# A fused recurrent block and six attention layers on one core: the half step's instructions in a new order on all five engines

## The reference, cut to what matters

```python
xn = layernorm(x)                      # x: (2, 1024, 128)
s = recurrent(xn)                      # 192 hidden channels, scan over the tokens
y = xn
for i in range(6):                     # 16 heads of 64, windows of 32 tokens
    q, k, v = split(shift_tokens(y) @ Wqkv[i])        # 128 -> 3 x 1024
    q, k = rotary(l2norm(q) * qs[i]), rotary(l2norm(k) * ks[i])
    att = softmax(mask(q @ k.T * 8)) @ v   # each window looks at itself and the one before
    y = att @ Wo[i] + y
    h = layernorm(shift_tokens(y)) @ W1[i] + b1[i]    # 128 -> 2 x 341
    y = (h[:341] * gelu(h[341:])) @ W2[i] + b2[i] + y
out = x + s * silu(y)
```

## Time and profile before

| | us |
|---|---|
| median of 3 runs | 1771.38 |
| the runs | 1769.56, 1771.38, 1780.35 |
| the profiled execution, its own time | 1782.22 |
| its span | 1780.4 |
| TensorE busy | 1595.2 (90%) |
| VectorE busy | 1417.4 (80%) |
| GpSimd busy | 1367.1 (77%) |
| ScalarE busy | 1070.2 (60%) |

### The profile page before, as it was taken

One profiled execution on the slowest core, in us unless ns is written; L12 is line 12 of the kernel. 1 busy time (PEld: TensorE's weight loads), 2 busy tenths in 40 slices (PEclk: granted clock), 3 DMA queues, 4 the chain that ended last, 5 costly groups with the idle time before them and its releaser, 6 DMA issues.

```text
span 1780.4 us, 76109 instructions
## 1 busy us (share of the span) xinstructions
PE 1595.2 (90%) x32303; PEld 1327.5 (75%) x32303; DVE 1417.4 (80%) x2163; ACT 1070.2 (60%) x2132; POOL 1367.1 (77%) x1321
## 2 busy tenths in 40 slices
PE   6888898999999898998999888899899999999986
PEld 3767777777777787777877777777777777777865
DVE  7777788778778687778888777888877899998964
ACT  5545565656656565566665656666665666666752
POOL 7877888878779677778877778887787967767732
PEclk9999999999999899899999999999999999999988
DMA  4334332434333334232343333243333333332330
GB/s 135 88 79 106 76 88 67 102 88 109 72 90 76 82 86 117 66 84 71 91 104 91 91 80 88 68 114 89 96 80 81 85 74 71 85 77 62 75 88 27
DMA packets 217857, 151.20 MB, mean 85 GB/s; under 512 B 144557, under 2 KB 164657, under 8 KB 217521
## 3 DMA queue, kind: packets, MB, share of 16 engines
q1 hardware_dynamic: 217520, 146.33, 33.7%
HBM read 27.50 MB, written 1.05 MB: 16 GB/s over the span
## 4 chain that ended last, share of the span: by engine, by line
PE 32%; SPq 29%; DVE 17%; DMA 10%; issue 8%; ACT 2%; POOL 1%; DVEq 0%; ACTq 0%; POOLq 0%
DMA v_win<-v_new 10%; SPq L608 9%; PE ps_pv L868 7%; SPq L606 4%; DVE ss L1523 4%; SPq L603 4%; DVE v_new L1534 4%; PE ps_pv L890 3%; SPq L294 3%; PE ps_qn L777 3%; SPq L574 3%; PE ps_tr L802 2%; PE ps_s L842 2%; PE ps_qn L779 2%; PE ps_qn L778 2%
## 5 line engine op out<-in xcount | busy, mean ns | idle before, releaser
L1976 POOL TENSOR_TENSOR qk<-qk,t 128x1024 f32<-128x1024 f32 x192 | 459.0, 2392 | 135.1 <-DVE qk L1513 134.9
L1510 DVE TENSOR_TENSOR t<-ps_qn,tab 128x512 f32<-128x512 f32 x384 | 263.7, 687 | 149.3 <-ACT sq L1164 142.3
L1988 POOL TENSOR_TENSOR qkr<-qk,rinv 128x1024 f32<-128x1024 f32 x192 | 364.0, 1917 | 7.6 <-POOL rinv L1968 0.2
L777 PE MATMUL ps_qn<-w_hi,xs_hi 128*128 128x512 f32 x576 | 268.0, 465 | 46.1 <-DVE v_new L1534 35.6
L1164 ACT ACTIVATE sq<-ps_qn 128x512 f32<-128x512 f32 x384 | 231.5, 603 | 89.8 <-PE ps_qn L779 89.4
L868 PEld LDWEIGHTS ps_pv<-pT,v_win 64*64 64x64 f32 x12288 | 208.5, 140 | 91.9 <-issue 91.6
L1513 DVE TENSOR_TENSOR qk<-ps_qn,tab 128x512 f32<-128x512 f32 x384 | 261.4, 681 | 0.0
L868 PE MATMUL ps_pv<-pT,v_win 64*64 64x32 f32 x12288 | 230.7, 225 | 12.3 <-issue 10.4
L779 PE MATMUL ps_qn<-w_hi,xs_lo 128*128 128x512 f32 x576 | 236.2, 410 | 0.0
L778 PE MATMUL ps_qn<-w_lo,xs_hi 128*128 128x512 f32 x576 | 235.8, 409 | 0.4 <-issue 0.4
L1534 DVE COPY v_new<-ps_qn 128x512 f32<-128x512 f32 x184 | 119.6, 686 | 133.1 <-DMA v_win<-v_new 127.6
(11 more groups left out here) (169 smaller groups left out, 3002.5 us busy)
## 6 DMA issues: line engine op xcount, KB each, us to landing
v_win<-v_new SPq DMA_DIRECT2D x576, 128.0 KB, 2.4
v_win<-v_new SPq DMA_DIRECT2D x192, 64.0 KB, 2.1
v_win<-v_win SPq DMA_DIRECT2D x188, 64.0 KB, 2.0
kT<-kT SPq DMA_DIRECT2D x84, 128.0 KB, 3.1
w_raw<-in_Wqkv SPq DMA_DIRECT2D x18, 512.0 KB, 4.7
rot<-in_rot SPq DMA_DIRECT2D x48, 128.0 KB
wo<-in_Wo SPq DMA_DIRECT2D x6, 512.0 KB, 4.3
x<-x SPq DMA_DIRECT2D x48, 56.0 KB
```

What stands on the lines that cost most here:

```text
L777: mm(ps_qn[bank][:, :], xs_hi[b][:, :], w_hi[:, part], start=True, stop=False)
L1510: v.tensor_tensor(t2[:, part].rearrange("p (h s d) -> p h s d", s=2, d=DH // 2), swapped, tab[:, 2 * k + 1:2 * k + 2, :].rearrange("p o (s ...
L1976: g.tensor_tensor(qk[b][:, part], qk[b][:, part], t2[:, part], ALU.add).then_inc(added[b], 1)
L1988: g.tensor_tensor(qkr[b][:, part].rearrange("p (h d) -> p h d", d=DH), qk[b][:, part].rearrange("p (h d) -> p h d", d=DH), rinv[b][:, k * ...
```

## The change

- **v in two places**: `v_new` has two buffers for each stream, by the step's parity. `evac_v` is ScalarE's now, in all steps, and waits for the moves of tile i-2 instead of those of tile i-1.
- **Half step in a new order**: on TensorE the mask stands earlier and `scores` and both parts of `probs_v` follow each other at the end of the half. The mixed transpose stands just before them.
- **Output projection half a step later**: the projection of stream 1 of tile i-3 is done in half (i, 0), that of stream 0 of tile i-2 in half (i, 1), with the down products of tile i-4.
- **Up products** are done in half (i, 0) and fill the banks of `pv_order` instead of those of `qn_order`. All mixed transposes fill `tr_order`.
- **Engines**: `low_x` (L2037 before), `low_fxn` (L2006) and `normalise_mid` (L2012) are VectorE's instead of GpSimd's. On GpSimd `scale_probs` stands before the second `add`. On ScalarE `inverse_root` is the last of a half instead of the first.
- **SyncE** issues `move_v` of the half before first, then the shift of `xmid`.
- The drain is rewritten to match.

The core of the diff:

```diff
@@ pv_order
     for b in range(B):
+        if has_out(i, 1 - b):
+            order += [("out", 1 - b)]
+        if b == 0 and valid(i - 4):
+            order += [("up", c) for c in range(3)]
         if valid(i - 2):
-            order += [("pv", b, f) for f in range(2)]
-        if valid(i - 2) or (b == 0 and valid(i - 5)):
-            order += [("out", b)]
+            order += [("pv", b, h) for h in range(2)]
...
-        v_new = per_stream("v_new", [P, INNER])
+        v_new = [[sb(f"v_new{b}_{n}", [P, INNER]) for n in range(2)] for b in range(B)]
...
@@ SyncE, half
                     if b == 0:
+                        carry_k(i, 1)
+                        move_v(i - 1, 1)
+                        shift_xmid(i)
                         load_out_weights(i)
-                        shift_xmid(i)
+                    else:
+                        carry_k(i + 1, 0)
+                        move_v(i, 0)
...
-                    carry_k(i, b)
-                    move_v(i, b)
...
@@ TensorE, half
                     qkv(i, b, (0, 1))
...
-                    probs_v(i, b, 0)
+                    out_projection(i, 1 - b)
+                    if b == 0:
+                        ffn_up(i, 0)
+                    transpose_keys(i, b)
                     mask(i, b)
-                    probs_v(i, b, 1)
                     qkv(i, b, (2, 3))
...
+                    rec_hidden(i, b)
+                    rec_gate_projection(i, b)
                     if b == 0:
-                        ffn_down(i)
-                        transpose_keys(i, b)
+                        ffn_up(i, 1)
...
+                    transpose_qk(i, b, 0)
+                    rec_output(i, b)
+                    rec_rates(i, b)
+                    transpose_qk(i, b, 1)
+                    qkv(i, b, (4, 5))
...
+                    if b == 0:
+                        ffn_up(i, 2)
+                    if not i.first:
                         transpose_mixed(i, b)
...
                     scores(i, b, 0)
                     scores(i, b, 1)
+                    probs_v(i, b, 0)
+                    probs_v(i, b, 1)
...
@@ ScalarE, evac_v
-                    if i.n > 1:
-                        return
                     bank, n = fill(qn_order, i, ("qkv", b, c))
                     act.wait_ge(qn_full[bank], n)
-                    if c == 4:
-                        after_first(act, v_moved[b], i.n * V_MOVE, i)
-                    f(v_new[b][:, (c - 4) * COLS:(c - 3) * COLS], ps_qn[bank][:, :], ACT.Copy).then_inc(qn_done[bank], 1)
+                    if c == 4 and valid(i - 2):
+                        act.wait_ge(v_moved[b], (i.n - 1) * V_MOVE)
+                    f(v_new[b][i.n % 2][:, (c - 4) * COLS:(c - 3) * COLS], ps_qn[bank][:, :], ACT.Copy).then_inc(qn_done[bank], 1)
...
@@ VectorE, half
+                        if c == 1:
+                            take_out(i, 1 - b)
+                            row_sums(*soft)
+                            row_recips(*soft)
+                            if b == 0:
+                                rec_driving(i - 1, 1)
+                            else:
+                                normalise_rows(i)
...
-                        evac_v(i, b, 4)
-                        evac_v(i, b, 5)
-                        if i.t == 4:
+                        ffn_gate(i, 2)
+                    if not (i.first and b == 0):
+                        low_x(*next_tile(i, b))
+                    if b == 0:
+                        mid_variance(i)
+                    else:
+                        low_fxn(i - 3)
...
@@ GpSimd, half
-                    if b == 1:
-                        low_fxn(i)
                     add(i, b, 0)
-                    if b == 1:
-                        normalise_rows(i)
...
+                    scale_probs(*softmax_tile(i, b))
                     add(i, b, 1)
-                    scale_probs(*softmax_tile(i, b))
-                    if not early(*next_tile(i, b)):
-                        low_x(*next_tile(i, b))
```

More of the change, by code:

```diff
@@ L139, in tr_order @@
         if valid(i - 1):
-            order += [("qk", b, f) for f in (2, 3)]
-        if b == 1 and has_mixed(i, b):
-            order += ["mixed"]
-        if valid(i - 1):
-            order += [("qk", b, f) for f in (0, 1)]
+            order += [("qk", b, f) for f in (2, 3, 0, 1)]
+        if has_mixed(i, b):
+            order += [("mixed", b)]
     return order
@@ L193, in fill @@
 def fill(order, i, what):
-    steps = sum(len(order(Step(0, k))) for k in range(min(i.n, STEPS)))
-    n = steps + (order(i).index(what) if i.n < STEPS else DRAIN_FILLS[order].index((i.n, what)))
+    first = sum(len(order(Step(0, k))) for k in range(min(i.n, STEPS)))
+    n = first + (order(i).index(what) if i.n < STEPS else DRAIN_FILLS[order].index((i.n, what)))
     return n % 2, n // 2 + 1
@@ L206, in down_of, with mixed_of @@
     return "down" if i.n >= STEPS else ("out", 0)
+def mixed_of(i, b):
+    return "mixed" if i.n >= STEPS else ("mixed", b)
 def build(nc, a):
@@ L568, in shift_xmid @@
                         return
[L569 to L570 removed]
+                    wait_fill(sp, pv_done, pv_order, i - 1, ("out", 0))
+                    wait_fill(sp, pv_done, pv_order, i, ("out", 1))
                     k, to = mid_slot(n), slice(0, HALF)
@@ L743, in transpose_mixed @@
                         return
-                    order, full, done, banks = mixed_ring(b)
-                    bank, n = fill(order, i, "mixed")
-                    ring_free(pe, done, bank, n)
+                    bank, n = fill(tr_order, i, mixed_of(i, b))
+                    ring_free(pe, tr_done, bank, n)
                     t, s = next_tile(i, b)
@@ L1124, in evac_mixed @@
                         return
-                    order, full, done, banks = mixed_ring(b)
-                    bank, n = fill(order, i, "mixed")
-                    act.wait_ge(full[bank], n)
+                    bank, n = fill(tr_order, i, mixed_of(i, b))
+                    act.wait_ge(tr_full[bank], n)
                     t, s = next_tile(i, b)
-                    m = i - 4
+                    m = i - 3
                     if valid(t):
```

555 lines of the change are left out of this document (240 added, 315 removed).

## The result

| | median us | runs |
|---|---|---|
| before | 1775.87 | 4, 1769.56 to 1781.08 |
| after | 1968.49 | 4, 1962.57 to 1975.02 |

The ratio is 1.109 (95% interval 1.103 to 1.115): **slower by 11%**. The forecast was 1680, range 1600 to 1755, and its chance of slower was 0.09, given to a mechanism that did not occur. The profiled execution after took 1975.0, its span 1972.9.

The account below looks back on a forecast made before the run. Bound: a loop through v's copy, SyncE's queue and DMA, 35.1 us a step. New step 31.1 + 0.4 + 1.5 = 33.0; 39 x 2.1 plus 8 recurrent x 1.2 gives 92 us less: 1680, range 1600 to 1755.

Parts of the forecast that it names:

- the loop: Each step cycled through VectorE's copy of v, SyncE's queue and the move DMAs, 35.1 us on average; two buffers break it.
- Tiled products together: Scores and `probs_v` in one run on TensorE: six tiling switches become three a half, saving 0.7 us a step.
- TensorE's work of 31.1 us a step: Floor of an ordinary step: TensorE's measured 31.8 us less 0.7 for fewer tiling switches.
- The wait for rotations: In half (i, 1) TensorE waits for late VectorE before the last chunk: 2.0 us lost, 1.5 counted.
- the third gate's wait: Near the end of half (i, 0) TensorE waits 0.4 us for the third gate, behind the 2.2 us of `ss`.
- The recurrent steps: Eight steps with the recurrence, 38.7 us each before: gain between 0 and 2.3 us, middle 1.2 taken.
- Rival 2: VectorE's four moved places wait for GpSimd's running instructions, 3.9 us a step: 1816 us, slower; chance 0.09.
- Rival 3: ScalarE's loaded half with b = 0 runs 2 us late, a new loop keeping the step at 35.1: 1771 us; chance 0.10.
- Rival 1: ScalarE and VectorE hand on in time, only TensorE's work of 31.1 us a step is left: 1597 us; chance 0.14.

Follow-up runs that it names:

- the best version: Kernel before with v in two places and the mask behind both parts of `probs_v`, plus ScalarE copying v in all steps: 1646.4 us, ratio 0.929.
- The kernel at 1792: Kernel after with the scores and last up chunk ahead of the fifth chunk, and the recurrence's matmuls behind both query transposes: 1792.2 us, ratio 1.011.
- the kernel at 1675: Kernel before with v in two places and the mask behind both parts of `probs_v` instead of between them, VectorE still copying v: 1675.4 us, ratio 0.941.

## Why the prediction was wrong

**v in two places** was right: the loop was the bound, it is gone, and alone it gives 89 us. That the time of this part alone (1687) is near the forecast for the whole (1680) is chance.

**"Tiled products together"** is the step that failed. Its working counted what the edit takes away, changes of tiling, and that price was of the right size (0.2 us each, 0.11 taken). It had no term for what a run of 256 small matmuls does by itself: stops of 1.35 us, 122.6 us in all, 2.6 a step. (Set against the kernel before, which had stops too, all "issue" rows grew by 92 us, 2.0 a step.) The earlier trace rows showed the rate that makes them (64 tiled matmuls from 857.35 to 858.41), and the kernel before already stopped inside the scores. I read past this row of the waits of before:

```profile
PE ps_s L842 <- issue: 27.3, 18, 2.6
```

Shown by three edits: cutting the run takes most of the stops away in two ways, lengthening it in the old order makes them. The last section shows what they are.

**TensorE's work of 31.1 us a step** took the clock of before for granted. Measured: 33.0 at a clock of 0.92. TensorE stops more often now, and the clock falls behind stops. One case, after: the transposes end, TensorE waits 1.91 us for VectorE, and the mean clock of the stretch behind the wait is 0.50, that ahead of it 1.00:

```profile
577.63 1.04 PE L804 MATMUL ps_tr<-ident,qkr 128*128 128x128 f32 x8
580.59 0.47 PE L779 MATMUL ps_qn<-w_hi,xs_hi 128*128 128x512 f32 x1 [1.91 <-DVE qk L1488]
```
```profile
575.00:579.00 4.00, 3.67 (x25) 2.97 (x23) 3.82 (x6) 2.86 (x6) 3.47 (x2) 1.00 0.30 68
581.80:585.20 3.40, 3.40 (x106) 2.67 (x109) 2.36 (x2) 2.21 (x7) 2.41 (x1) 0.50 0.01 2
```

Of the twelve such stretches between 580 and 900 us, each began behind a stop of 0.8 to 2.3 us, seven in front of the fifth chunk and five in `probs_v`. The reverse does not hold: half of the 26 stops of that size in the same time had no fall behind them. Stretches at the lower clock: 104.7 us before, 314.8 after, 46.5 in the best version. (The 97% above was the mean granted clock, 0.971; the time at full clock was 94% of the span.) The Trainium skill (TensorE: Matmul & The Clock Gate, Part 1: The HAM clock gate) describes a clock that follows how busy the engine has been; the trace agrees, 1.00 and 0.50 around one wait.

**The wait for rotations** was right in place and size: 95.7 / 47 = 2.0 us a step, forecast 2.0. Counting only 1.5 of it, because of pauses that would overlap, was wrong: the pauses come at the other end of the half. Its cause stands in TensorE's order: in a half with b = 1 the kernel before had the output projection and two up chunks between the fourth and the fifth chunk, and after has only transposes there. The scores moved into this place cover most of it again (27.3 us are left).

Together for an ordinary step, from the forecast 33.0: clock and busy time +1.9, stops in `probs_v` +2.6, wait for rotations +0.5, the third gate's wait -0.3 (it has 2.9 us in all), and 0.6 of small waits not assigned: 38.3.

**The recurrent steps** were forecast to gain 1.2 and lost 7.9 each. The ordinary loss of 3.2 is in this; beyond it, hidden and gate stand directly behind the third and fourth chunk in TensorE's order and wait for the rotations of these very chunks (23.3 + 8.8 us in eight steps, 4.0 each). Moving them gave 11 us on after, within the scatter, and 18 on the kernel with the scores early, so the rows overstate what their place in the order costs. I had looked at VectorE's sum there and not at what stands behind what on TensorE.

**Rival 2** (GpSimd holds VectorE) did not happen: `xs_lo` takes 0.292 at the median, forecast near 0.3, and once 2.05 at most. **Rival 3** had a wait for ScalarE, which has 2% of the chain. **Rival 1** spoke of a floor of 31.1 us of work, and the work itself came to 33.0.

**Why the new order stays worse even when mended.** The kernel at 1792 has TensorE idle for 235 us of its span (1794.7 - 1559.7), the one at 1675 for 132. The difference of 103 is about the size of three rows: 57.3 for the bank of the last up product (`DVE hid`), 26.7 for the queries' evacuation, and 26.3 against 10.7 for rotations; the other rows rise and fall and about cancel. So "up products in `probs_v`'s banks" has a row of its own, but no run puts them back into their old banks, so its price is not shown. It is one of three waits that exchange: each edit that took one away made others grow more. Whether some order inside this design avoids all three stays open; three were tried. So do some 14 us at the start and the drain, which no run separates.

## What to carry to other kernels

Price a run of small, fast instructions by its number and not only by its duration: here, in runs of 128 and 256 matmuls of 16 ns with their weight loads, TensorE stood still for more than a microsecond at a time, mostly beyond the first 64. So put small matmuls between large ones, where they also cover waits. When a change has a part that breaks a measured loop and a part that reorders the rest, time the first alone: here it gave 5%, and with the copies on a less loaded engine 7%, while the rest, order and engines together, cost 281 us. And do not carry a TensorE time from one order to another without asking where TensorE will stop, since the clock falls behind stops.

## What the hardware showed that I had not expected

The instruction stream has a rate. The page's instruction queues moved 4.23 + 0.63 = 4.86 MB for 76,065 instructions: 64 bytes each.

```profile
span 1972.9 us, 76065 instructions
...
q8 instruction: 258, 4.23, 0.9%
q14 instruction: 77, 0.63, 0.1%
```

A packet of the first queue holds 4.23 MB / 258 = 16.4 kB, 256 instructions, 128 matmuls with their loads; 258 packets are about TensorE's 2 x 32,303 instructions, and with `probs_v` done twice they are 351. In the trace's records such a packet takes 1.09 us at the median. The scores' 256 instructions ran in 1.83 us (1022.38 - 1020.55). In the trace of after, each of the 90 stops of over 0.5 us inside tiled runs ended 1.2 to 1.8 us after a packet had landed (one landed at 1023.59, and TensorE went on at 1024.95), where only 11% of the other tiled matmuls start. In full-array work the same 256 instructions last much longer (six matmuls, 12 instructions, take 1.57 us).

The places of the stops settle what they are. Number all 66,135 instructions of TensorE in the trace from 0 in the order of time, and take each number's remainder by 256: 100 of the 102 "issue" stops of over 0.5 us fall on the remainders 193 to 196, and none of the 70 waits for semaphores of that size does. That is one place in each 256 instructions, so TensorE stops where one packet of instructions ends and the next begins (the program's first instructions stand outside this count, hence 193 and not 0, I take it). It does so when it has run through a packet quickly: of the 97 such borders that it reached less than 2.5 us after passing the one before, 87 had a stop; of the 149 that it reached after more than 3.5 us, four. How the fetch works inside stays open, and the time of one packet does not decide everything: in the kernel at 1675, 25 of 98 borders reached after 3.5 to 5 us had a stop. The Trainium skill (Runtime: NRT & Kernel Launch, Instruction fetch mechanics) gives the same blocks of 256 instructions and calls the cost of crossing from one to the next mostly hidden; for tiled matmuls the trace does not agree, with 122.6 us of stops.

Second, adding 80 us of useless work made the kernel 35 us faster, because it broke the run of small matmuls; about as much in front of the fifth chunk changed nothing (1965).
